# Routing table built from one comparison per tile with the token number multiplied in on ScalarE, late shared tiles ahead of the first expert sums, and context values loaded behind the second tile's rows

## The chip, the cores and the metric

One core of one Trainium2 chip runs the whole program in a single launch. The metric is device time in microseconds (us), the median of three runs. Every matrix lies in the on-chip memory with 128 partitions; TensorE (PE) multiplies, VectorE (DVE), ScalarE (ACT) and GpSimd (POOL) do the rest, SyncE (SP) issues most of the plain transfers, and POOL issues the indirect ones (gathers by a table of row numbers).

## The reference

The input x is 8 batches of 256 tokens with 256 features, so 2048 tokens. Four residual layers follow one another:

```
x = x + tanh(g_xattn[0]) * cross_attention(layernorm(x), context, mask)       (8 heads, 77 keys)
x = x + tanh(g_ffn[0])   * mixture(layernorm(x))                              (below)
x = x + tanh(g_xattn[1]) * self_attention_with_context(layernorm(x), context) (16 heads, 77 + 256 keys)
x = x + tanh(g_ffn[1])   * lora_mixture(layernorm(x))                         (8 experts, 2 a token)
```

The mixture of the second line has 64 experts of inner width 176. Each token takes 8 of them, by sigmoid scores and a choice of groups; its result is the weighted sum of their 8 outputs plus the output of one shared expert of width 352. The reference computes it densely; the kernel computes only the chosen experts.

## The kernel before, in words

Work is in tiles of 128 tokens: NT = 16 tiles, TOPK = 8 choices a token, so 128 pairs of a tile and a choice. The stages that the change touches are these.

**Shared expert, early part.** The first NSE = 10 tiles of tokens go through the shared expert while the routing table is being made. One step per tile (`s_step`) on PE: two up products (one for each half f of the inner width), the two transposes of the hidden values of the tile before, the transposes of the next tile's input, and the down product of the tile before. ACT does the silu and two copies of each half, copies hT (the transposed hidden values) and xT (the transposed input), and scales the down product into yC (`s_y_out`, line 1034). POOL multiplies silu and up values (`shared_h`) and adds yC to x.

**Routing table.** Each of the 2048 x 8 choices has got a slot number; slot / 128 is a block (one expert's batch of 128 rows), slot % 128 a place in it. The table idx (place x block -> token number) is made with matmuls: for a tile t and choice k, PE adds ohP^T x ohB to one PSUM bank. ohB (128 tokens x 192 blocks, fp16) is 1 where the token's block is, made for all 8 choices by one comparison (line 2083). ohP (128 tokens x 128 places, fp16) holds the token number where the token's place is, made by 8 instructions that compare and multiply (line 2088). These have a ring of OHS = 4 tiles: DVE can be at most four tiles ahead of PE, which counts each of its 128 matmuls on `b_ohu`. On PE the order is written out by hand: two tiles of the table behind each of the shared steps 6 to 9 (FILL_AT = 6), then transposes of the last hidden tile, table tile 8, the last down product, and tiles 9 to 15. When the bank is whole, three DVE instructions turn it into idx (lines 2097 to 2099), `b_idx` is raised, and POOL starts gathering (line 769).

**Routed experts.** 191 blocks, one step each (`c_step`): POOL gathers 128 rows of the normalised input by idx, PE transposes, multiplies up, transposes, multiplies down, ACT stores y to memory. SP loads the experts' weights into 8 slots as they come free.

**Late part.** The last NSL = 6 tiles of tokens go through the shared expert behind the last block, in 12 half steps m = 0 to 11 (`late_up`, `late_silu`, `c_hidden`, `late_down`); `late_hidden` on DVE does the product hC (line 2116) and the copy hT (line 2119) of the half steps that it is given, and `late_add` adds the finished tile into x (line 2150). When every y row is in memory POOL gathers, for each token tile, its 8 rows (line 786, yg): first 16 gathers for both tiles of batch 0, then 5 for batch 1. DVE sums the 8 rows (`d_reduce`, line 2247, two halves of a tile) and adds them into x (`d_sum`). Then come the statistics and the norm (`d_ve`, `d_rstd`, `d_norm`) with which the third layer starts. The order on DVE is written by hand: half steps 0 and 1, bproj, clearing half of qP (line 2395), 2 and 3, the other half, 4 and 5, and then by `FIRST_LATE` half steps between the four `d_reduce` of batch 0.

On SP the third layer's loads follow the last late row load: `load_raw(0)`, `load_raw(1)` (512 KB each), `load_keys(0)` (308 KB), a wait for cleared v1 and qP, `load_values(0)` and `load_values(1)` (two transfers each, in pieces of 64 bytes, line 628), `load_keys(1)`, which waits for POOL to have used the keys before, and more. PE first needs the values in `d_values` of batch 0.

qP and v1 are also cleared earlier, in six pieces during the first blocks (`clear`, lines 2123 to 2129), each of which counts on `d_zero`.

Of the kernel before, what the change touches and what calls it, by code (L numbers as in the profile page):

```python
# [14 lines left out]
P = 128  # L15
# [80 lines left out]
def bass_flamingo(nc, A, out):  # L96
    with ExitStack() as ctx:  # L97
# [5 lines left out]
        def sem(name):  # L103
            return ctx.enter_context(nc.semaphore(name))
# [44 lines left out]
        with ExitStack() as region:  # L149
# [32 lines left out]
            blkH = s("blkH", [P, NT * TOPK, 2], FP16)  # L182
            parF = s("parF", [P, NT * TOPK])
            iotaP = s("iotaP", [P, P], FP16)
# [109 lines left out]
        with ExitStack() as region:  # L294
# [23 lines left out]
        b_slot = sem("b_slot")  # L318
        b_sel, b_pos, b_eb, b_er, b_oh, b_ohu, b_idx = (
            sem(n) for n in ("b_sel", "b_pos", "b_eb", "b_er", "b_oh", "b_ohu", "b_idx"))  # L320

# [196 lines left out]
        def _(sp):  # L518
# [105 lines left out]
            def load_values(b):  # L624
                if b >= 2:
                    sp.wait_ge(d_pv, H1 * (b - 1))
                for e in range(2):
                    sp.dma_start(v1[0:NKEY, b % 2, 0, :, 3 * e, :], A["ctx"][b][:, D:2 * D].rearrange("k (p e d) -> e k p d", p=HP1, e=2)[e]).then_inc(d_cv[b % 2], 16)
# [15 lines left out]
            load_keys(0)  # L644
            sp.wait_ge(d_zero, ZERO_PIECES)
            load_values(0)
            load_values(1)
# [326 lines left out]
        def _(act):  # L974
# [81 lines left out]
            s_copy_xT(0, 0)  # L1056
            pairs(act, s_step, n=NSE)
            s_copy_hT(NSE - 1)
            s_y_out(NSE - 1, 1, NSE // 2 - 1)


# [205 lines left out]
        def _(pe):  # L1267
# [144 lines left out]

            def onehots(t, r):
                for k in range(TOPK):
                    pe.wait_ge(b_oh, TOPK * t + k + 1)
                    start = isinstance(t, int) and t == 0 and k == 0
                    stop = isinstance(t, int) and t == NT - 1 and k == TOPK - 1
                    mm(ps[:, POS[1], 0:NBLK], ohP[:, r, k, :], ohB[:, r, k, :], start, stop).then_inc(b_ohu, 1)

# [415 lines left out]
        def _(dve):  # L1835
# [239 lines left out]
            own.link(dve.tensor_scalar(slotI[:], slotI[:], P - 1, None, ALU.bitwise_and))  # L2075
            own.step(dve.tensor_copy(parF[:], slotI[:]))
            own.link(dve.tensor_copy(blkH[:], blkI[:].unsqueeze(2).broadcast_to([P, NT * TOPK, 2])))
            TWOS = [P, TOPK, NBLK // 2, 2]
            end()

            def onehots(t, r):
                after(dve, b_ohu, TOPK * (t - OHS + 1))
                dve.tensor_tensor(ohB[:, r, :, :].rearrange("p k (n a) -> p k n a", a=2),
                                  iotaB[:].rearrange("p (n a) -> p n a", a=2).unsqueeze(1).broadcast_to(TWOS),
                                  blkH[:, bass.ds(TOPK * t, TOPK), :].unsqueeze(2).broadcast_to(TWOS), ALU.is_equal)
                for k in range(TOPK):
                    u = TOPK * t + k
                    dve.tensor_scalar(ohP[:, r, k, :], iotaP[:], col(parF, u), col(id1, t), ALU.is_equal, ALU.mult).then_inc(b_oh, 1)

            for t in range(OHS):  # L2090
                onehots(t, t)
            with dve.Fori(1, NT // OHS) as i:
                for r in range(OHS):
                    onehots(OHS * i + r, r)
            dve.wait_ge(b_ohu, TOPK * NT)
            begin()
# [296 lines left out]
            dve.tensor_scalar(bproj[:], bproj[:], tg[:, 1:2], None, ALU.mult).then_inc(d_gate, 1)  # L2393
            for h in range(2):
                dve.memset(qP[h * (P // 2):(h + 1) * (P // 2), :, 1 - h, :].bitcast(F32), 0.0).then_inc(d_zero, 1)
                late_hidden(2 * h + 2, 2 * h + 3)

            FIRST_LATE = ((6, 7), (), (8, 9), (10, 11))
            for r in range(TB):
# [171 lines left out]
```

## Time and profile before

| what | us |
|---|---|
| median of 3 runs | 1512.27 (1512.11 to 1514.17) |
| the profiled execution, its own time | 1514.72 |
| its span in the trace | 1512.9 |
| PE busy | 1364.1 (90%) |
| DVE busy | 861.2 (57%) |
| ACT busy | 692.9 (46%) |
| POOL busy | 514.6 (34%) |
| mean granted TensorE clock | 0.943 of full |

The stages by the trace's clock: first attention to about 104 us, routing and early shared tiles to 216 us, routed blocks to about 715 us, late shared tiles and expert sums to 775 us, third layer to about 1200 us, fourth layer to the end. "Granted clock" 1.00 is 2.4 GHz and 0.50 is 1.2 GHz. A stretch in which PE is busy for all of its time says little about DVE; where PE has gaps, the engine that ends each gap sets the time.

### The profile page before, as it was taken

The page shows a single profiled execution, that of the slowest core. Times are in us where ns is not written, and L with a number is a line of the kernel's source. Part 1 is how long each engine was busy: PE and PEld are TensorE (multiplying, and loading weights), DVE is VectorE, ACT ScalarE, POOL GpSimd, SP SyncE. Part 2 cuts the span into 40 slices and gives each one's busy share as a digit, 9 for nine tenths or more (in the row PEclk, how much of TensorE's full clock was granted, in tenths as well). Part 3 has the DMA queues.
Part 4 walks back from the last instruction along what each step waited for, and adds up shares of the span by engine and source line. Part 5 has one row for each costly group of instructions (what it writes and reads, how often), then busy time and mean ns, then how long its engine had stood idle before and what let it go on. Part 6 is the DMA issues. An engine that isn't in the chain of part 4 may idle for free. (4 is left out here: it accounts for less than half of the span.)

```text
span 1512.9 us, 30501 instructions
## 1 busy us (share of the span) xinstructions
PE 1364.1 (90%) x8093; PEld 1070.4 (71%) x8093; DVE 861.2 (57%) x2301; ACT 692.9 (46%) x1847; POOL 514.6 (34%) x570
## 2 busy tenths in 40 slices
PE   4988969999999999999566799999998899999998
PEld 3876636777777777777344567776765799999997
DVE  6878964333333333333337567667678576666666
ACT  2444303444444444444024577677776444444443
POOL 1001323333333333331554477656662111111110
PEclk8877969999999999999787899999999899999999
DMA  4016115768566557643422122221120000000000
GB/s 104 0 54 170 26 33 161 219 191 241 160 202 185 174 161 218 192 115 93 128 86 64 57 57 65 59 66 50 44 87 22 10 13 15 15 14 14 14 7 15
DMA packets 107710, 136.12 MB, mean 90 GB/s; under 512 B 29843, under 2 KB 91635, under 8 KB 107603
## 3 DMA queue, kind: packets, MB, share of 16 engines
q1 hardware_dynamic: 64643, 61.15, 13.9%
q0 software_dynamic: 15456, 48.62, 12.0%
q10 hardware_dynamic: 27504, 25.05, 4.9%
q8 instruction: 53, 0.87, 0.2%
q14 instruction: 54, 0.44, 0.1%
HBM read 102.75 MB, written 32.01 MB: 89 GB/s over the span
## 5 line engine op out<-in xcount | busy, mean ns | idle before, releaser
L769 POOL DMA_INDIRECT xg<-n_rows,idx x191 | 181.1, 948 | 314.9 <-DVE wS L2110 218.5
L1269 PE MATMUL ps<-wgu,xT 128*128 x764 | 260.6, 464 | 0.6 <-ACT xT L1070 0.6
L1269 PE MATMUL ps<-wdn,hT 88*128 x764 | 198.4, 382 | 2.5 <-DVE hT L2119 2.5
L2287 DVE TENSOR_REDUCE nmx<-ps 128x1 f32<-128x333 f32 x256 | 127.1, 498 | 123.3 <-PE ps L1269 118.8
L1147 ACT ACTIVATE pD<-ps,nmx 128x333 f32<-128x333 f32 x256 | 139.2, 546 | 98.6 <-DVE nmx L2287 75.6
L2116 DVE TENSOR_TENSOR hC<-sg,ps 128x176 f32<-128x176 f32 x203 | 68.5, 337 | 185.1 <-ACT sg L1080 162.2
L2119 DVE COPY hT<-ps 88x256 f32<-88x256 f32 x203 | 85.4, 421 | 152.4 <-issue 86.9
L1269 PEld LDWEIGHTS ps<-wgu,xT 128*128 128x128 f32 x764 | 130.8, 191 | 42.5 <-issue 2.0
L1587 PE MATMUL ps<-ident,pD 128*128 128x128 f32 x768 | 130.9, 281 | 28.2 <-DVE pT L2293 16.0
L786 POOL DMA_INDIRECT yg<-y_rows,slotG x128 | 123.4, 964 | 93.3 <-ACT pD L1147 33.7
L1080 ACT ACTIVATE sg<-ps 128x176 f32<-128x176 f32 x191 | 60.6, 318 | 185.4 <-PE ps L1269 179.2
L1269 PEld LDWEIGHTS ps<-wdn,hT 88*128 88x128 f32 x764 | 130.8, 191 | 13.9 <-issue 3.0
L1089 ACT ACTIVATE yC<-ps,wS 128x256 f32<-128x256 f32 x191 | 90.6, 474 | 106.1 <-issue 65.8
L1587 PEld LDWEIGHTS ps<-ident,pD 128*128 128x128 f32 x768 | 98.8, 144 | 39.9 <-issue 21.0
L1269 PE MATMUL ps<-kM,qP 128*128 128x334 f32 x256 | 108.6, 426 | 5.2 <-ACT pD L1147 4.8
L1350 PEld LDWEIGHTS ps<-ident,xg 128*128 128x128 f32 x414 | 59.1, 144 | 64.8 <-issue 34.2
L1355 PE MATMUL ps<-ident,hC 128*88 128x128 f32 x446 | 85.6, 277 | 19.9 <-DVE hC L2116 13.9
L1269 PE MATMUL ps<-pT,v 128*32 128x256 f32 (+1 forms) x768 | 97.7, 390 | 0.6 <-ACT pT L1154 0.6
L2434 DVE TENSOR_TENSOR gg<-sl,ps 128x256 f32<-128x256 f32 x128 | 53.0, 420 | 79.3 <-ACT sl L1235 78.5
L1235 ACT ACTIVATE sl<-ps 128x256 f32<-128x256 f32 x128 | 48.3, 383 | 107.6 <-PE ps L1269 104.2
L1355 PEld LDWEIGHTS ps<-ident,hC 128*88 128x88 f32 x446 | 53.0, 124 | 53.9 <-DVE hC L2116 21.7
L1350 PE MATMUL ps<-ident,xg 128*128 128x128 f32 x414 | 80.7, 277 | 9.2 <-DMA xg<-n_rows,idx 6.1
(310 smaller groups left out, 3084.7 us busy)
## 6 DMA issues: line engine op xcount, KB each, us to landing
y_rows<-yC ACTq DMA_DIRECT2D x191, 128.0 KB
wgu<-in_wgu SPq DMA_DIRECT2D x64, 352.0 KB
wdn<-in_wdn SPq DMA_DIRECT2D x64, 176.0 KB
xg<-n_rows,idx POOLq DMA_INDIRECT x191
kraw<-in_kD SPq DMA_DIRECT2D x8, 308.0 KB
x<-in_x SPq DMA_DIRECT2D x4, 512.0 KB, 4.8
n_rows<-nB SPq DMA_DIRECT2D x4, 512.0 KB, 3.4
xg<-n_rows SPq DMA_DIRECT2D x16, 128.0 KB
```

The source lines that it names most:

```text
L769: pool.indirect_dma_start(out=xg[:, b % XS, :], out_offset=None, in_=n1_rows, in_offset=bass.IndirectOffsetOnAxis(ap=idx[:, b:b + 1], axis ...
L786: pool.indirect_dma_start(out=yg[:, q, k, :], out_offset=None, in_=y_rows, in_offset=bass.IndirectOffsetOnAxis(ap=slotG[:, u:u + 1], axis= ...
L1080: act.activation(sg[:, n % 2, :], ps[:, 2 + n % 2, 0:I0], ACT.Silu).then_inc(c_silu, 1)
L1089: act.activation(yC[:, (n - 1) % YS, :], ps[:, 6 + (n - 1) % 2, 0:D], ACT.Copy, scale=wS[:, (n - 1) % XS:(n - 1) % XS + 1]).then_inc(c_y, 1)
L1147: act.activation(pD[:, k % AHEAD, :], ps[:, score_bank(k), 0:NK1], ACT.Exp, bias=nmx[:, k:k + 1], accum_out=den[:, k // TB // HG1, head_of ...
L1269: return pe.matmul(o, lhsT, rhs, start=start, stop=stop, **kw)
L1350: last = pe.transpose(ps[:, bank, at + c * P:at + (c + 1) * P], xg[:, slot, c * P:(c + 1) * P], ident[:])
L1355: last = pe.transpose(ps[0:IC, bank, at + c * P:at + (c + 1) * P], hC[:, slot, c * IC:(c + 1) * IC], ident[:])
L1587: last = pe.transpose(ps[:, 5 + k % 2, c * P:(c + 1) * P], pD[:, k % AHEAD, at:at + P], ident[:])
L2116: dve.tensor_tensor(hC[:, n % 2, :], sg[:, n % 2, :], ps[:, 2 + n % 2, I0:GU], ALU.mult).then_inc(c_h, 1)
L2119: dve.tensor_copy(hT[:, n % 2, :, :], ps[0:IC, 4 + n % 2, 0:2 * P].rearrange("p (c n) -> p c n", c=2)).then_inc(c_hT, 1)
L2287: dve.tensor_reduce(nmx[:, k:k + 1], ps[:, score_bank(k), 0:NK1], AX, ALU.max, negate=True).then_inc(d_mx, 1)
```

## The change

Three edits. In the routing table the comparison of places is one DVE instruction for the 8 choices of a tile (`rows_of_a_tile`, 128 x 1024 fp16), ahead of the comparison of blocks; ACT multiplies the result in place by the token number (`numbered`, one instruction a tile, 128 x 1024 fp16, scale from id1). On ACT's queue two `numbered` stand behind each shared step 6 to 9, one behind the last hT copy, and the rest behind the last yC. PE waits once a tile for both, and counts once a tile. In the late part the two clearings of qP are gone, half steps 2 to 7 stand ahead of the first `d_reduce`, 8 behind the first, 9 to 11 behind the second, none behind the third and fourth. SP waits for the 8 gathers of batch 0's second tile (`k_ld[1]`) ahead of `load_values(0)`.

```diff
-            parF = s("parF", [P, NT * TOPK])
+            parH = s("parH", [P, NT * TOPK, 2], FP16)
...
             load_keys(0)
             sp.wait_ge(d_zero, ZERO_PIECES)
+            sp.wait_ge(k_ld[1], 16 * TOPK)
             load_values(0)
...
-            pairs(act, s_step, n=NSE)
+
+            def numbered(n):
+                rows = ohP[:, n % OHS, :, :].rearrange("p k n -> p (k n)")
+                act.wait_ge(b_oh, 2 * n + 1)
+                act.activation(rows, rows, ACT.Copy, scale=id1[:, n:n + 1]).then_inc(b_ohn, 1)
+
+            for t in range(2):
+                s_step(t, t, 0)
+            with act.Fori(1, FILL_AT // 2) as i:
+                for r in range(2):
+                    s_step(2 * i + r, r, i)
+            for t in range(FILL_AT, NSE):
+                s_step(t, t % 2, t // 2)
+                for s in range(2):
+                    numbered(2 * (t - FILL_AT) + s)
             s_copy_hT(NSE - 1)
+            numbered(2 * (NSE - FILL_AT))
             s_y_out(NSE - 1, 1, NSE // 2 - 1)
+            for n in range(2 * (NSE - FILL_AT) + 1, NT):
+                numbered(n)
...
             def onehots(t, r):
+                pe.wait_ge(b_oh, 2 * t + 2)
+                pe.wait_ge(b_ohn, t + 1)
                 for k in range(TOPK):
-                    pe.wait_ge(b_oh, TOPK * t + k + 1)
...
-                    mm(ps[:, POS[1], 0:NBLK], ohP[:, r, k, :], ohB[:, r, k, :], start, stop).then_inc(b_ohu, 1)
+                    last = mm(ps[:, POS[1], 0:NBLK], ohP[:, r, k, :], ohB[:, r, k, :], start, stop)
+                last.then_inc(b_ohu, 1)
...
-            own.step(dve.tensor_copy(parF[:], slotI[:]))
+            own.step(dve.tensor_copy(parH[:], slotI[:].unsqueeze(2).broadcast_to([P, NT * TOPK, 2])))
...
+            def rows_of_a_tile(out, iota, number, t, n):
+                twos = [P, TOPK, n // 2, 2]
+                return dve.tensor_tensor(out.rearrange("p k (n a) -> p k n a", a=2),
+                                         iota[:].rearrange("p (n a) -> p n a", a=2).unsqueeze(1).broadcast_to(twos),
+                                         number[:, bass.ds(TOPK * t, TOPK), :].unsqueeze(2).broadcast_to(twos), ALU.is_equal)
+
             def onehots(t, r):
-                after(dve, b_ohu, TOPK * (t - OHS + 1))
-                dve.tensor_tensor(ohB[:, r, :, :].rearrange("p k (n a) -> p k n a", a=2),
...
-                for k in range(TOPK):
-                    u = TOPK * t + k
-                    dve.tensor_scalar(ohP[:, r, k, :], iotaP[:], col(parF, u), col(id1, t), ALU.is_equal, ALU.mult).then_inc(b_oh, 1)
+                after(dve, b_ohu, t - OHS + 1)
+                rows_of_a_tile(ohP[:, r, :, :], iotaP, parH, t, P).then_inc(b_oh, 1)
+                rows_of_a_tile(ohB[:, r, :, :], iotaB, blkH, t, NBLK).then_inc(b_oh, 1)
...
-            for h in range(2):
-                dve.memset(qP[h * (P // 2):(h + 1) * (P // 2), :, 1 - h, :].bitcast(F32), 0.0).then_inc(d_zero, 1)
-                late_hidden(2 * h + 2, 2 * h + 3)
-
-            FIRST_LATE = ((6, 7), (), (8, 9), (10, 11))
+            late_hidden(2, 3, 4, 5, 6, 7)
+
+            FIRST_LATE = ((8,), (9, 10, 11), (), ())
```

## Rows read from the trace of the kernel before

**Rows 1.** Busy time by stretch: us, then PE, PEld, DVE, ACT, POOL, granted clock, DMA share, GB/s
```profile
200.00:212.00 12.00, 8.39 (x36) 3.75 (x36) 12.00 (x43) 0.00 (x0) 0.00 (x0) 0.50 0.01 1
320.00:700.00 380.00, 374.38 (x1791) 274.35 (x1790) 123.13 (x449) 158.68 (x447) 139.24 (x147) 1.00 0.61 180
732.00:740.00 8.00, 3.83 (x14) 2.23 (x13) 2.54 (x3) 0.32 (x1) 5.86 (x8) 0.94 0.94 281
740.00:748.00 8.00, 2.91 (x8) 1.63 (x6) 0.81 (x2) 0.00 (x0) 6.17 (x7) 0.50 0.57 132
```
**Rows 2.** Groups by line and form: count | busy us, mean ns | idle before
```profile
L2088 DVE TENSOR_SCALAR ohP<-iotaP,parF,id 128x128 f16<-128x128 f16 x128 | 33.7, 332 | 0.0
...
L2083 DVE TENSOR_TENSOR ohB<-iotaB,blkH 128x1536 f16<-128x1536 f16 x16 | 15.4, 961 | 0.0
...
L1175 ACT CAST lT_h<-maskS 128x1024 fp32r<-128x1024 f32 x8 | 8.3, 1040 | 1.0 <-DVE maskS L2347 1.0
...
L1034 ACT ACTIVATE yC<-ps,tg 128x256 f32<-128x256 f32 x10 | 4.7, 474 | 14.7 <-PE ps L1269 14.7
...
L1102 ACT COPY xT<-ps 128x256 f32<-128x256 f32 x6 | 2.2, 372 | 0.0
```
**Rows 3.** Timeline of PE, 172 to 213 us: start, us, what, [idle before]
```profile
172.39 2.65 PE L1269 MATMUL ps<-wguS,xT 128*128 128x352 f32 x4
...
178.89 1.49 PE L1269 MATMUL ps<-ohB,ohP 128*128 128x192 f16 x16
180.21 1.38 PE L1269 MATMUL ps<-wguS,xT 128*128 128x352 f32 x4
...
184.99 1.49 PE L1269 MATMUL ps<-ohB,ohP 128*128 128x192 f16 x16
...
192.20 0.60 PE L1355 MATMUL ps<-ident,hC 128*88 128x128 f32 x4
...
193.90 1.97 PE L1269 MATMUL ps<-wdnS,hT 88*128 88x256 f32 x8
...
211.22 1.90 PE L1269 MATMUL ps<-ohB,ohP 128*128 128x192 f16 x8 [0.75 <-DVE ohP L2088]
```
**Rows 4.** Timeline of ACT at the start of the table
```profile
166.88 0.47 ACT L1034 ACTIVATE yC<-ps,tg 128x256 f32<-128x256 f32 x1 [1.24 <-PE ps L1269]
```
**Rows 5.** Timeline of DVE at the end of the table
```profile
213.16 0.36 DVE L2097 TENSOR_SCALAR isz<-ps 128x192 f32<-128x192 f32 x1 [0.43 <-PE ps L1269]
```
**Rows 6.** Timeline of POOL: the first block gather; the first and 21st row gather
```profile
216.14 1.10 POOL L769 DMA_INDIRECT xg<-n_rows,idx  x1 [18.29 <-issue]
...
722.32 0.95 POOL L786 DMA_INDIRECT yg<-y_rows,slotG  x1 [28.52 <-DMA y_rows<-yC]
...
747.40 0.95 POOL L786 DMA_INDIRECT yg<-y_rows,slotG  x1 [0.30 <-issue]
```
**Rows 7.** Timeline of DVE in the late part
```profile
721.04 1.76 DVE L2395 MEMSET qP<- 64x2048 f32 x1 [0.37 <-issue]
722.73 0.27 DVE L2116 TENSOR_TENSOR hC<-sg,ps 128x176 f32<-128x176 f32 x1
...
746.07 0.42 DVE L2119 COPY hT<-ps 88x256 f32<-88x256 f32 x1 [7.63 <-remote]
...
753.46 1.87 DVE L2247 TENSOR_REDUCE ysum<-yg 128x128 f32<-128x1024 f32 x1
...
769.33 0.48 DVE L2150 SCALAR_TENSOR_TENSOR x<-ps,tg,x 128x256 f32<-128x256 f32 x1 [1.22 <-PE ps L1269]
```
**Rows 8.** Timeline of ACT in the late part and in the third layer
```profile
751.68 0.32 ACT L1109 ACTIVATE sg<-ps 128x176 f32<-128x176 f32 x1 [13.70 <-remote]
...
828.06 0.48 ACT L1154 COPY pT<-ps 128x384 f32<-128x384 f32 x1 [4.94 <-remote]
```
**Rows 9.** Timeline of SP, the value loads
```profile
733.38 6.69 SPq L628 DMA_DIRECT2D v<-in_ctx  x4
```
**Rows 10.** DMA of 740 to 744 us: SP's queue q1: packets, MB, share of 16 engines
```profile
q1 hardware_dynamic: 1314, 0.08, 23.1%
```

More of the change, by code:

```diff
@@ L318, in bass_flamingo @@
         b_slot = sem("b_slot")
-        b_sel, b_pos, b_eb, b_er, b_oh, b_ohu, b_idx = (
-            sem(n) for n in ("b_sel", "b_pos", "b_eb", "b_er", "b_oh", "b_ohu", "b_idx"))
+        b_sel, b_pos, b_eb, b_er, b_oh, b_ohn, b_ohu, b_idx = (
+            sem(n) for n in ("b_sel", "b_pos", "b_eb", "b_er", "b_oh", "b_ohn", "b_ohu", "b_idx"))
         s_x = [sem(f"s_x{r}") for r in range(2)]
@@ L2075, in _ @@
             own.link(dve.tensor_scalar(slotI[:], slotI[:], P - 1, None, ALU.bitwise_and))
-            own.step(dve.tensor_copy(parF[:], slotI[:]))
+            own.step(dve.tensor_copy(parH[:], slotI[:].unsqueeze(2).broadcast_to([P, NT * TOPK, 2])))
             own.link(dve.tensor_copy(blkH[:], blkI[:].unsqueeze(2).broadcast_to([P, NT * TOPK, 2])))
-            TWOS = [P, TOPK, NBLK // 2, 2]
             end()
-            def onehots(t, r):
-                after(dve, b_ohu, TOPK * (t - OHS + 1))
-                dve.tensor_tensor(ohB[:, r, :, :].rearrange("p k (n a) -> p k n a", a=2),
-                                  iotaB[:].rearrange("p (n a) -> p n a", a=2).unsqueeze(1).broadcast_to(TWOS),
-                                  blkH[:, bass.ds(TOPK * t, TOPK), :].unsqueeze(2).broadcast_to(TWOS), ALU.is_equal)
-                for k in range(TOPK):
-                    u = TOPK * t + k
-                    dve.tensor_scalar(ohP[:, r, k, :], iotaP[:], col(parF, u), col(id1, t), ALU.is_equal, ALU.mult).then_inc(b_oh, 1)
+            def rows_of_a_tile(out, iota, number, t, n):
[3 more added lines that the diff above has]
+                                         number[:, bass.ds(TOPK * t, TOPK), :].unsqueeze(2).broadcast_to(twos), ALU.is_equal)
+            def onehots(t, r):
+                after(dve, b_ohu, t - OHS + 1)
+                rows_of_a_tile(ohP[:, r, :, :], iotaP, parH, t, P).then_inc(b_oh, 1)
+                rows_of_a_tile(ohB[:, r, :, :], iotaB, blkH, t, NBLK).then_inc(b_oh, 1)
             for t in range(OHS):
@@ L2094, in _ @@
                     onehots(OHS * i + r, r)
-            dve.wait_ge(b_ohu, TOPK * NT)
+            dve.wait_ge(b_ohu, NT)
             begin()
```

## The prediction

> **What bounds the kernel now.** I read the busy times by stretch first, then each engine's timeline around the two edited places, then the groups for prices, and last the DMA.
>
> The routed blocks between the two places are PE's: 374 of 380 us busy at full clock [rows 1]. Their 12 matmuls a block (1791 in 380 us) make a step of about 2.5 us. They start when the first gather starts, and everything behind them waits for them. So a microsecond won ahead of the first gather at 216.14 [rows 6] is won at the end, as is one won between the last block and the start of the third layer.
>
> In the routing table DVE sets the end: from 200 to 212 us it is busy for all 12 us, ACT for none, and PE, at half clock, waits before each tile for ohP [rows 1, 3]. A tile costs DVE one ohB and 8 ohP. The last matmuls start at 211.22 and run 1.90, so PE is done at 213.12 and DVE goes on at 213.16 [rows 3, 5]. Earlier, however, PE and not DVE is the pace: while shared steps run, the sixteen matmuls of two tiles run without a wait in 1.49 us, and one turn (step and two tiles) takes 184.99 - 178.89 = 6.10 us [rows 3]. DVE is up to four tiles ahead there. Its 47 us of comparisons are thus on the path only in the tail.
>
> In the late part nothing is busy: PE 2.91 of 8 us in 740 to 748, ACT none [rows 1]. The last half step's add is at 769.33 [rows 7]. The waits that matter bear no engine's name: ACT stands 13.70 us before the silu at 751.68 and DVE 7.63 us before the copy at 746.07, both "remote", both waiting for PE matmuls long issued [rows 7, 8]. They fall into the 21 gathers that POOL issues from 722.32 to 747.40 at 1.25 us each [rows 6], and into the time in which the DMA engines are 0.94 busy [rows 1].
>
> **The change, part by part: the table.** On DVE the 8 instructions of 332 ns fall away: 33.7 + 15.4 = 49.1 us busy over 16 tiles is 3.1 us a tile now [rows 2]. One instruction of 1024 elements comes. Its nearest row is ohB, the same form with 1536 elements in 961 ns [rows 2]. In proportion that is 0.64 us, and it can't be more than the 0.96 of the larger one; I take 0.65. A tile then costs DVE about 1.6 us. The preparation cast grows from 128 to 256 outputs, below 0.1 us. A rule of the Trainium skill speaks against this edit: VectorE: DVE Perf Modes, "The perf-mode tier table", says that a 16-bit operation on two tensors makes two results a cycle where a tensor_scalar makes four. By it alone the new comparison would be the slower one for each element. The 332 ns for 128 elements show that most of the old price was a fixed part paid eight times.
>
> On ACT the product comes, 128 x 1024. The nearest row is the cast of 1024 elements, 1040 ns; a scale read from a column adds 474 - 372 = 0.10 us [rows 2], so 1.14, and 1.05 at the pitch of one behind another. That those rows are 32-bit leaves a bound below: half of it, 0.57, if 16-bit data ran twice as fast. The Trainium skill (ScalarE: Activation LUTs, "What ACT_TABLE_LOAD costs") gives 0.833 ns an element for fp32 and bf16 alike, and about 93 ns for each column operand, which would make 1.13.
>
> Now the path, on PE and ACT together. **Start:** ACT is free at 166.88 + 0.47 = 167.35 [rows 4]. Two products: 168.5 and 169.55. PE needs 0.66 for the second eight matmuls (half of 1.49, less the tail), so shared step 7 starts at 170.2 instead of 172.39 [rows 3]: -2.2 us. **Three turns (steps 7, 8, 9):** the products stand on ACT behind the yC that needs PE's down product, so when PE has ended the step it waits 0.5 for yC, 1.14 and 1.05 for two products, and runs 0.66 more: 3.4 us in place of the 1.33 between the start of the sixteen and the next step. +2.1 each, +6.2 us. The cover under which the comparisons ran is given up here: DVE's time is not saved in these turns, since PE did not wait for it. **Tail:** from the transposes at 192.20 to 213.12 it is 20.9 us [rows 3]. Then: transposes 0.45, hT copy 0.6, product 1.14, eight matmuls 0.66, down product 1.8, yC 0.5, product 1.14, six more at 1.05, last eight 0.66, and four handovers of 0.15: 13.9. That is at full clock. At half clock, which rows show for this stretch before (0.50 in 200 to 212, [rows 1]), the eight matmuls take 1.3 us a tile and become the pace of the last seven: 2.1 more, 16.0. I take the half clock, as PE stands still for as long as before: -4.9 us. DVE's ring of four leaves 1.6 + 1.14 + 1.3 a tile round a loop of four tiles, no bound. Sum of the table: -2.2 + 6.2 - 4.9 = **-0.9 us**.
>
> **The late part.** Each clearing stands 1.76 us in DVE's queue and makes the hC behind it wait: the one at 721.04 ends where hC starts at 722.73 [rows 7], which at the steps' pitch would have started some 1.2 us sooner. Twice 1.2 us. qP is zero already and bproj stays, so nothing else moves with them. That puts PE and DVE one half step of 2.5 us ahead when the long waits start at about 733. If these stay as they are, DVE has half step 8 at 752 where it had 7. Behind it: 1.1 us for step 8, the second reduce with its sum and statistics 2.7 (a reduce is 1.87 us, [rows 7]), 9 to 11 at 2.5 each less what overlaps, about 6, and the last two reduces with sum and statistics 4.6. I come to the last add at 767.4 instead of 769.3 + 0.5: **-2.4 us**. The reduces no longer stand between the half steps, but they are still DVE's work.
>
> The four value transfers take SP 6.69 us from 733.38 [rows 9] and lie among the row gathers. Alone in 740 to 744 they take 23.1% of the engines, 0.9 us, for 0.08 MB in 1314 packets [rows 10]; I put as much again for the 4 us before, by the same number of pieces. Moved behind the second tile's gathers, they give back **1.7 us** of a full DMA. At their new place, about 745, they need some 10 us and are waited for by the first `d_values`, beyond 800. On SP the load_keys(1) behind them waits anyway for POOL at about 774, and the next loads stand behind that, so the wait costs nothing unless the late part ends 15 us earlier.
>
> Total: -0.9 - 2.4 - 1.7 = -5.0 us. The sum is made against the profiled execution, 1514.72 us (span 1512.9 and 1.8 around it). That is 2.4 above the median of the three runs, 1512.27. So 1507.3. About 0.2%, 3 us, is what a measurement of this kernel can tell from no change.
>
> **Rivals.** (a) *The long waits go.* If the value packets are what holds PE's results between 733 and 752, the half steps run on at 2.5 us, end at about 749, and the second tile's rows (last gather issued at about 741, landed by 745) set the last two reduces: the add at about 754, -15.5 us instead of -4.1, total -16, so 1496. For it: the waits fall into the fullest DMA. Against it: ACT waits 4.94 us "remote" before 828.06 [rows 8] while only gathers run, and the wait up to 751.68 has 8 us behind the last value packet. The gathers alone make such waits. 0.14.
>
> (b) *It cancels.* The products behind yC cost what the tail gives, the late part gives the 2.4 us and the third layer's start eats some of it, where POOL's next eleven gathers hold PE again. 1512.3 less 0 to 3. 0.28.
>
> (c) *Slower.* PE's gap of 2.7 us after each shared step, split by eight matmuls, lets the clock fall to 0.50 during steps 7 to 9. The up product at 172.39 takes 2.65 us at half clock, the one at 180.21 takes 1.38 [rows 3]; over the part of a step that runs before the clock is back I put 1.7 us. With all three +5, the table is at +4.2 and the whole at 0; it is slower from there if the late part gives less than 2, for instance because the values now collide with the last five gathers and hold PE in half steps 9 to 11: 1512.3 + 4. For it: PE is idle more than a quarter of each turn. Against: each gap stands beside 4.8 us without one (6.10 - 1.33), and step 7 was slow before as well. The Trainium skill, TensorE: Matmul & The Clock Gate, names 1.2 GHz as the state after idling; it gives (c) its mechanism. 0.11.
>
> (d) *The comparison is not made at the fast rate* because of its broadcast operands: ohB has the same and took 961 ns for 1536, so I leave it out.
>
> **How the numbers follow.** My forecast, -3 to -9, has 0.47; (a) 0.14, (b) 0.28, (c) 0.11. Faster by over 3 us: nearly all of the forecast case and (a), 0.58. Within: 0.30. Slower: 0.12. The range takes in the bounds: the tail at full clock (-2.1 more), 16-bit products at 0.57 us (-8), and on the other side the clock's fall (+5). 1498 to 1514.
>
> **What would show it.** Right: ohP as one instruction of about 0.65 us, product 1.14 us, gap on PE of about 1.65 us before table tiles 2, 4, 6 with ACT's product as releaser; first block gather at about 215; ACT's wait before 752 still there; last late add about 767 less the table's gain. Wrong: a first gather before 212 (products cheaper, or overlapped) or after 218 (clock), or the "remote" waits gone.

## The result: slower by 0.33% where 0.3% faster was forecast

The changed kernel takes 1519.47 us (median of 6, 1516.63 to 1521.99), the kernel before, run beside it, 1513.41 (6 runs, 1512.11 to 1515.30): ratio 1.0033, 95% interval 1.0020 to 1.0046. The forecast was 1507.3 within 1498 to 1514, so both the sign and the range are wrong. The profiled execution is the lowest of the six, 1516.63 with a span of 1514.9; against the 1512.9 of before the two traces hold 2.0 us of the 6.1 by which the medians differ. By stage: everything ahead of the table is 2.5 us shorter (DVE's first comparison at 163.57, before 166.04), the table 3.1 longer, the way from the first block gather to the third layer's first norm (nS) 0.6 shorter, and what stands behind it 2.0 longer (741.4, before 739.4). The edits leave the last of these alone and touch the first by one cast, so what the two executions differ by there can't be laid to them.

Busy time by stretch of the changed kernel (columns as in [rows 1]), and the head of its page:

```profile
200.00:212.00 12.00, 9.47 (x57) 8.18 (x58) 5.79 (x8) 7.45 (x9) 0.72 (x1) 0.68 0.01 1
320.00:700.00 380.00, 374.32 (x1793) 274.63 (x1792) 123.12 (x448) 159.05 (x449) 138.86 (x147) 1.00 0.61 180
732.00:740.00 8.00, 4.39 (x12) 2.41 (x12) 0.34 (x1) 0.32 (x1) 6.09 (x7) 0.59 0.68 245
740.00:748.00 8.00, 2.07 (x4) 1.17 (x4) 0.81 (x2) 0.00 (x0) 6.14 (x9) 0.50 0.59 118
```
```profile
span 1514.9 us, 30328 instructions
...
PE 1357.9 (90%) x8093; PEld 1070.2 (71%) x8093; DVE 835.3 (55%) x2187; ACT 709.1 (47%) x1863; POOL 512.6 (34%) x570
```

DVE has 26 us less to do (861.2 before), and nothing came of it. The routed blocks are the same. In the table DVE is no longer busy all the time, but the end did not come earlier. In 740 to 748 us there is still next to nothing at work.

Groups by line and form in 160 to 216 us of the changed kernel (count | busy us, mean ns | idle before):

```profile
L2102 DVE TENSOR_TENSOR ohB<-iotaB,blkH 128x1536 f16<-128x1536 f16 x16 | 15.7, 983 | 0.0
L2102 DVE TENSOR_TENSOR ohP<-iotaP,parH 128x1024 f16<-128x1024 f16 x16 | 11.0, 686 | 24.0 <-PE ps L1287 23.8
```
```profile
L1062 ACT ACTIVATE ohP<-ohP,id 128x1024 f16<-128x1024 f16 x16 | 17.3, 1139 | 1.1 <-DVE ohP L2102 1.1
```

The prices were right: 0.69 us for the comparison (0.65 forecast), 1.14 for the product (1.14). The 24 us of idle time in front of the comparisons, released by PE, say that DVE's saving has become waiting. PE's timeline shows why:

```profile
165.71 0.83 PE L1287 MATMUL ps<-ohB,ohP 128*128 128x192 f16 x8 [2.20 <-DVE ohB L2102]
...
167.59 1.44 PE L1287 MATMUL ps<-ohB,ohP 128*128 128x192 f16 x8 [1.04 <-ACT ohP L1062]
168.82 2.61 PE L1287 MATMUL ps<-wguS,xT 128*128 128x352 f32 x4
...
172.07 2.11 PE L1287 MATMUL ps<-wguS,xT 128*128 128x352 f32 x4
...
177.82 0.82 PE L1287 MATMUL ps<-ohB,ohP 128*128 128x192 f16 x8 [1.69 <-ACT ohP L1062]
178.85 0.82 PE L1287 MATMUL ps<-ohB,ohP 128*128 128x192 f16 x8 [0.22 <-ACT ohP L1062]
179.51 1.38 PE L1287 MATMUL ps<-wguS,xT 128*128 128x352 f32 x4
...
186.15 0.82 PE L1287 MATMUL ps<-ohB,ohP 128*128 128x192 f16 x8 [1.69 <-ACT ohP L1062]
187.19 1.41 PE L1287 MATMUL ps<-ohB,ohP 128*128 128x192 f16 x8 [0.22 <-ACT ohP L1062]
188.39 2.50 PE L1287 MATMUL ps<-wguS,xT 128*128 128x352 f32 x4
...
197.76 1.06 PE L1373 MATMUL ps<-ident,hC 128*88 128x128 f32 x4
200.62 1.44 PE L1287 MATMUL ps<-ohB,ohP 128*128 128x192 f16 x8 [1.81 <-ACT ohP L1062]
201.86 3.13 PE L1287 MATMUL ps<-wdnS,hT 88*128 88x256 f32 x8
206.68 0.82 PE L1287 MATMUL ps<-ohB,ohP 128*128 128x192 f16 x8 [1.69 <-ACT ohP L1062]
207.72 6.02 PE L1287 MATMUL ps<-ohB,ohP 128*128 128x192 f16 x48 [0.22 <-ACT ohP L1062]
```

Each turn ends with 1.69 us for the product behind yC and 0.22 for the second, as forecast. From the up product of step 7 to the last transposes it is now 197.76 - 168.82 = 28.9 us, 19.8 before (172.39 to 192.20, [rows 3]): +9.1. The waits make 3 x 1.91 = 5.7 of that. Another 0.3 a turn goes because the sixteen matmuls no longer run close behind the down product and one another (a turn's waits thus cost 2.2). The other 2.5 us are the granted clock at half: 0.7 in step 7's second up product (2.11 us, 1.42 before), 0.6 in the eight matmuls at 187.19 (1.41 us, 0.82 at 178.85), 1.1 in the up product at 188.39 (2.50 us, 1.38 at 179.51 for the same four matmuls) and 0.1 behind 196.97. From the transposes to the end at 213.74 it is 16.0 us, as forecast. From DVE's first comparison (163.57, before 166.04) to isz it is 50.2 us where it was 47.1.

The two ends of the table and the late part, timelines of DVE, POOL and ACT of the changed kernel:

```profile
163.57 0.69 DVE L2102 TENSOR_TENSOR ohP<-iotaP,parH 128x1024 f16<-128x1024 f16 x1
164.18 1.48 DVE L2102 TENSOR_TENSOR ohB<-iotaB,blkH 128x1536 f16<-128x1536 f16 x1
...
213.78 0.36 DVE L2118 TENSOR_SCALAR isz<-ps 128x192 f32<-128x192 f32 x1 [1.42 <-PE ps L1287]
...
741.19 0.42 DVE L2140 COPY hT<-ps 88x256 f32<-88x256 f32 x1 [7.02 <-remote]
...
749.95 0.34 DVE L2137 TENSOR_TENSOR hC<-sg,ps 128x176 f32<-128x176 f32 x1 [7.95 <-ACT sg L1127]
...
751.48 1.88 DVE L2268 TENSOR_REDUCE ysum<-yg 128x128 f32<-128x1024 f32 x1
754.47 0.34 DVE L2137 TENSOR_TENSOR hC<-sg,ps 128x176 f32<-128x176 f32 x1 [1.11 <-ACT sg L1127]
...
764.80 3.66 DVE L2268 TENSOR_REDUCE ysum<-yg 128x128 f32<-128x1024 f32 x2
...
769.36 0.47 DVE L2171 SCALAR_TENSOR_TENSOR x<-ps,tg,x 128x256 f32<-128x256 f32 x1
```
```profile
216.76 1.10 POOL L770 DMA_INDIRECT xg<-n_rows,idx  x1 [10.45 <-issue]
...
746.47 0.95 POOL L787 DMA_INDIRECT yg<-y_rows,slotG  x1 [0.30 <-issue]
```
```profile
733.49 0.32 ACT L1127 ACTIVATE sg<-ps 128x176 f32<-128x176 f32 x1 [5.36 <-remote]
749.60 0.32 ACT L1127 ACTIVATE sg<-ps 128x176 f32<-128x176 f32 x1 [15.80 <-remote]
```

One more line of DVE before, which no row shows, and PE's up product of half step 7 in the changed kernel:

```profile
736.32 1.87 DVE L2247 TENSOR_REDUCE ysum<-yg 128x128 f32<-128x1024 f32 x1 [2.46 <-DMA yg<-y_rows,slotG]
```
```profile
734.68 2.55 PE L1287 MATMUL ps<-wguS,xT 128*128 128x352 f32 x4
```

The half steps run 2.4 us apart up to half step 5, earlier than before, and then stand in longer remote waits: 15.80 us where it was 13.70 [rows 8]. PE has done the up product of half step 7 at 737.2, and ACT starts its silu at 749.60, 12.4 us later. The lead goes in two places. In the wait it falls from 4.9 us (hT of half step 6 at 741.19, before 746.07 [rows 7]) to 2.1 (hC of half step 7 at 749.95, before 752.03). Behind the wait those 2.1 go too: before, one of the four sums was done inside the wait, at 736.32, and hC of half step 7 is followed by the last add 17.3 us later; now all four stand behind it, from 751.48 on, and it is 19.4 (e7 and e6, the old order and the new on another chip, have 18.5 and 20.6). The last add is at 769.36, before 769.33 [rows 7].

### The profile page after: what moved, and what is told of

It is laid out like the page before. It is cut to its first block and busy times, and to the rows that moved or that the text cites. A ratio compares the mean times of both kernels' runs of the same rounds, so it can differ in the third digit from the quotient of the medians.

```text
span 1514.9 us, 30328 instructions
## 1 busy us (share of the span) xinstructions
PE 1357.9 (90%) x8093; PEld 1070.2 (71%) x8093; DVE 835.3 (55%) x2187; ACT 709.1 (47%) x1863; POOL 512.6 (34%) x570
## 5 line engine op out<-in xcount | busy, mean ns | idle before, releaser
L1373 PEld LDWEIGHTS ps<-ident,hC 128*88 128x88 f32 x446 | 53.3, 125 | 50.9 <-DVE hC L2137 16.5
```

Of the source, the lines that this page charges most:

```text
L1373: last = pe.transpose(ps[0:IC, bank, at + c * P:at + (c + 1) * P], hC[:, slot, c * IC:(c + 1) * IC], ident[:])
```

## The experiments

Five sets of three or four kernels ran, each set on one chip and beside its own runs of the kernel before. Two sorts of chip were met, and nothing can be understood without them. On chips of sort W the kernel before takes 1513 to 1517 us and the traces have the long remote waits; the first result and sets 2 and 4 (two chips) are of this sort. On chips of sort F it takes 1483 us and no trace has a remote wait on ACT or DVE in the late part or the third layer; sets 1, 3 and 5 (two chips, 1 and 5 the same one). Ratios are against the kernel before on the same chip.

| run | set, sort | this, before (median us) | ratio (95%) |
|---|---|---|---|
| e1_table | 1 F | 1486.63, 1483.41 | 1.0026 (1.0014 to 1.0039) |
| e2_late | 1 F | 1474.64 | 0.9940 (0.9925 to 0.9955) |
| e3_values | 1 F | 1481.88 | 0.9989 (0.9979 to 1.0000) |
| e4_ahead | 1 F | 1467.74 | 0.9896 (0.9878 to 0.9914) |
| e5_changed | 2 W | 1521.84, 1516.51 | 1.0045 (1.0031 to 1.0059) |
| e6_late_values | 2 W | 1519.12 | 1.0012 (0.9995 to 1.0028) |
| e7_clearings | 2 W | 1517.82 | 1.0007 (0.9995 to 1.0019) |
| e8_order | 2 W | 1515.08 | 0.9996 (0.9983 to 1.0009) |
| e9_paced | 3 F | 1484.93, 1483.46 | 1.0008 (0.9997 to 1.0019) |
| e10_ahead_again | 3 F | 1466.62 | 0.9883 (0.9869 to 0.9897) |
| e11_ahead_paced | 3 F | 1471.06 | 0.9911 (0.9898 to 0.9924) |
| e12_changed_again | 4 W | 1517.31, 1513.77 | 1.0026 (1.0016 to 1.0036) |
| e13_paced_later | 4 W | 1510.95 | 0.9981 (0.9970 to 0.9992) |
| e14_ahead_table | 4 W | 1503.59 | 0.9930 (0.9915 to 0.9946) |
| e15_ahead_third | 4 W | 1500.14 | 0.9908 (0.9893 to 0.9924) |
| e16_changed_third | 5 F | 1481.96, 1482.75 | 0.9994 (0.9981 to 1.0007) |
| e17_ahead_paced_five | 5 F | 1468.98 | 0.9901 (0.9881 to 0.9920) |
| e18_ahead_fourth | 5 F | 1466.23 | 0.9879 (0.9855 to 0.9903) |

Two stretches of each profiled run tell the parts apart: the table, from DVE's first comparison to isz, and the way from the first block gather to nS. Each figure is of one execution.

| kernel | table | gather to nS, sort F | gather to nS, sort W |
|---|---|---|---|
| old table, old late part | 47.1 (before, e3, e7); 46.8 (e8) | 543.6 (e3, later values) | 557.3 (before), 558.1 (e7, no clearings), 559.2 (e8, new order) |
| changed table, old late part | 49.3 (e1) | 543.4 (e1) | |
| new late order | 47.0 (e2) | 538.5 (e2) | |
| new late order and values | 46.8 (e6) | 536.7 (e16) | 556.7 (changed), 557.7 (e12), 558.9 (e5), 561.9 (e6) |
| changed table in the changed kernel | 50.2, 49.9 (e5), 49.9 (e12), 50.9 (e16) | | |
| products one step ahead | 36.5, 35.6 (e4, e10), 36.4 (e14), 35.3 (e15), 36.2 (e18) | 537.0, 538.1, 535.4 (e4, e10, e18) | 556.9 (e15), 559.1 (e14, old late part) |
| paced gathers | | 539.7 (e9), 539.7 (e11), 537.5 (e17) | 545.4 (e13) |

### One part alone (e1, e2, e3)

The table's edit alone is the change without its hunk on SP and without the last one. The late order alone:

```diff
-            for h in range(2):
-                dve.memset(qP[h * (P // 2):(h + 1) * (P // 2), :, 1 - h, :].bitcast(F32), 0.0).then_inc(d_zero, 1)
-                late_hidden(2 * h + 2, 2 * h + 3)
-            FIRST_LATE = ((6, 7), (), (8, 9), (10, 11))
+            late_hidden(2, 3, 4, 5, 6, 7)
+            FIRST_LATE = ((8,), (9, 10, 11), (), ())
```

The values alone are one line on SP, `sp.wait_ge(k_ld[1], 16 * TOPK)`, ahead of `load_values(0)`.

> The kernel before with the routing table's edit alone (one comparison for the eight place rows, the products on ScalarE, PE waiting once a tile); the late order, its two clearings and the value loads as before. Theory A (the loss is in the table): in the profile of the changed kernel the table takes 50.2 us from the first comparison to the sums' end, against 47.1 before, so this kernel is 3 to 4 us slower than the kernel before, about 1516.5. Theory B (the table cancels, as I predicted, -0.9, and the loss is in the late part): within 1 us of the kernel before, 1512 to 1513.5.

> The kernel before with the late order alone: no second clearing of the queries' buffer, all late half steps up to 7 ahead of the first sums, 8 behind the first sum, 9 to 11 behind the second. Theory A (the late part is nearly neutral, since the profile of the changed kernel has its last add 0.9 us later behind the last block's product than before): 0 to +1.5 us, 1513 to 1515. Theory B (the late part holds the loss, because both sums of the second tile now stand behind the half steps that wait longest, at 764.80 for 3.66 us): +3 to +6 us. My prediction had -2.4.

> The kernel before with the later value loads alone. Theory A (the long waits go with the row gathers that POOL issues back to back and not with the value pieces): -1.7 to +0.5 us, with ACT's wait of over 10 us before about 750 still there. Theory B (the value pieces now collide with the last gathers or with the third layer's first loads, and this holds the loss): +2 to +4 us. My prediction had -1.7.

e1: ratio 1.0026, which is +3.9 us, and the table took 49.3 us. Theory A of e1 holds: this edit costs 3 to 4 us by itself (the absolute times in the expectations of this set are those of a chip of sort W). e2: 8.9 us faster, which neither theory had. On this chip the half steps of the late part are not held by anything but the queue of DVE. With the old order (e1), half step 6 stands behind a sum that waits for its rows:

```profile
729.72 1.87 DVE L2267 TENSOR_REDUCE ysum<-yg 128x128 f32<-128x1024 f32 x1 [4.21 <-DMA yg<-y_rows,slotG]
731.51 0.33 DVE L2136 TENSOR_TENSOR hC<-sg,ps 128x176 f32<-128x176 f32 x1
...
754.24 0.48 DVE L2170 SCALAR_TENSOR_TENSOR x<-ps,tg,x 128x256 f32<-128x256 f32 x1 [1.22 <-PE ps L1286]
```

With the new one two more half steps are done by then, and the last add comes at 750.06 in e2 though the first gather was 0.7 us later. The way to nS is 4.9 us shorter than in e1, 5.1 than in e3. The other 3.8 us of the 8.9 lie in no stretch that the trace explains: the profiled execution took 1478.5 us, the longest of e2's five. e3: -1.6 us, interval -3.1 to 0, where I had -1.7.

### The changed kernel on both sorts of chip (e5, e12, e16), and the late edits on sort W (e6, e7, e8)

e5, e12 and e16 are the changed kernel as it is. e6 is the kernel before with the late order and the values; e7 is the kernel before and leaves out only the two memsets; e8 keeps them and changes only the order:

```diff
+            late_hidden(6, 7)
-            FIRST_LATE = ((6, 7), (), (8, 9), (10, 11))
+            FIRST_LATE = ((8,), (9, 10, 11), (), ())
```

> The changed kernel itself, unaltered, beside new runs of the kernel before. The experiments on single parts ran on a chip on which the kernel before takes 1483.4 us and shows no wait of kind remote. Theory A (the parts add up: table +3.2, late order -8.8, values -1.5): 7 us faster than the kernel before on such a chip, and on a chip where the kernel before takes about 1513 us and shows the long remote waits, slower by about 6 as measured at first. Theory B (the parts collide with one another, whatever the chip): 4 to 6 us slower than before here too.

> The changed kernel once more, unaltered, to have it on the other kind of chip. Theory A (the parts add up): on a chip where the kernel before takes 1483 us, 7 us faster than it, 1476 to 1477, with all half steps 2.4 us apart and no remote wait; on a chip where it takes 1513 to 1516, +5 to +6 again. Theory B (the parts collide whatever the chip): slower than before on either.

> The changed kernel unaltered. Theory A (the parts add up on a chip without remote waits, where the kernel before takes 1483 us): about 1477, and the table alone takes 50 us there too. On a chip with them: +3.5 to +6 once more. Theory B (the sum does not hold): within 3 us of the kernel before, or slower, on a chip without remote waits.

> The late order and the later value loads together, the table as before. Theory A (the parts add up): -10.4 us on a chip without the remote waits; on a chip with them, +1 to +3, so that the table's +3.8 and this make the +6 measured at first. Theory B (the two late edits collide, since the values now wait for gathers that the late steps need too): clearly less than the sum of the two alone, -4 or worse.

> The kernel before without the second clearing of the queries' buffer, the late half steps in the old places. Theory A (each clearing held a half step for 1.2 us, as I predicted): -2 to -3 us. Theory B (DVE would wait there anyway for the first gathered rows): 0 to -1 us.

> The kernel before with the two clearings kept and only the order changed: half steps 6 and 7 ahead of the first sum, 8 behind it, 9 to 11 behind the second. Theory A (in the old order the half step behind a sum waits for the gathered rows, 4 us at 729 in a chip without remote waits, so the order carries most of the late gain): -5 to -7 us on such a chip, about 0 on a chip with remote waits. Theory B (the clearings carry it): 0 to -2 us.

On sort W the loss is there each time: +5.0, +6.8, +3.9 us by the ratios (about +6 was expected of e5, which holds, and +5 to +6 of e12, which came out a little lower). Beside the old table the late edits win nothing there: +1.8 (-0.8 to +4.2) together, as expected of e6, +1.1 (-0.8 to +2.9) the memsets, where both theories of e7 had a gain, -0.6 (-2.6 to +1.4) the order, as expected of e8, and gather to nS stays at 556.7 to 561.9. So on sort W the table's loss is what is left (3.1 us in the first trace, +3.9 by e1), with what e6 may add. One pair says otherwise: e14 and e15 below, one chip of sort W, differ only in the late edits, and with them it is 3.4 us less (1498.7 to 1501.4 against 1500.5 to 1505.0). Whether these edits win or lose up to 3 us on sort W is open; the 4.1 us that I forecast they do not win. On sort F the changed kernel comes to -0.9 us (-2.8 to +1.0), no change that can be told, where theory A of e16 had -6. Its late part did what e2's did: the first sum waits 2.32 us, and all is done at 750:

```profile
733.16 1.87 DVE L2268 TENSOR_REDUCE ysum<-yg 128x128 f32<-128x1024 f32 x1 [2.32 <-DMA yg<-y_rows,slotG]
734.95 0.33 DVE L2137 TENSOR_TENSOR hC<-sg,ps 128x176 f32<-128x176 f32 x1
...
750.07 0.47 DVE L2171 SCALAR_TENSOR_TENSOR x<-ps,tg,x 128x256 f32<-128x256 f32 x1
```

The medians of the parts do not add up there (+3.9 - 8.9 - 1.6 = -6.6 against -0.9), but the traces do. Between e1, which has the changed table, and e16, on the same chip, the way to nS is 6.7 us shorter (543.4, 536.7) and the table 1.6 longer (49.3, 50.9), so -5.1; e1 itself stands at +3.9, which makes -1.2. The term that is too large is e2's -8.9, of which its trace explains 5; where its median comes from stays open.

### The products one step ahead (e4, e10, e15, e18; with the old late part e14)

```diff
                 s_step(t, t % 2, t // 2)
-                for s in range(2):
-                    numbered(2 * (t - FILL_AT) + s)
+                for n in range(4) if t == FILL_AT else range(2 * (t - FILL_AT) + 2, 2 * (t - FILL_AT) + (3 if t == NSE - 1 else 4)):
+                    numbered(n)
             s_copy_hT(NSE - 1)
-            numbered(2 * (NSE - FILL_AT))
+            numbered(2 * (NSE - FILL_AT) + 1)
+            numbered(2 * (NSE - FILL_AT) + 2)
             s_y_out(NSE - 1, 1, NSE // 2 - 1)
-            for n in range(2 * (NSE - FILL_AT) + 1, NT):
+            for n in range(2 * (NSE - FILL_AT) + 3, NT):
                 numbered(n)
```

> The changed kernel with ScalarE's products moved one shared step ahead: four behind step 6, and behind each later step's output scaling the two of the next step, so that they run while PE does this step's tiles and the next up product; in the tail three of them ahead of the last output scaling. Theory A (what the table lost is PE's wait for the products at the end of each turn, 1.69 + 0.22 us, and the clock that falls with it): turns are back to about 6.1 us, PE's wait before tiles 2, 4, 6 is gone, the sums end at 196 to 202 instead of 213.8, and the kernel comes to 12 to 17 us below the changed kernel, 1502 to 1507. Theory B (the start of the gathers is not set by the sums but by something else that ends at about 213, or the products are the bound anyway): less than 4 us gained.

> The kernel before with the table's edit and its products one step ahead, the late order and the values as before. Theory A (the table by itself, with PE never waiting for a product during the shared steps, takes 36 us from the first comparison where the kernel before takes 47.1): 10 to 11 us below the kernel before, on either kind of chip. Theory B (part of the gain of the combined kernel came from the late order): less than 8.

> The products one step ahead in the changed kernel, for the third time, to have it on the other kind of chip. Theory A: on a chip with remote waits 13 to 14 us below the changed kernel, 8 to 9 below the kernel before; on one without, 15.7 to 16.8 below the kernel before as measured twice. Theory B (the earlier start is given back in the remote waits): within 4 us of the kernel before.

PE's timeline of e15, sort W:

```profile
169.36 2.18 PE L1288 MATMUL ps<-wguS,xT 128*128 128x352 f32 x4
...
176.27 1.38 PE L1288 MATMUL ps<-wguS,xT 128*128 128x352 f32 x4
...
181.05 1.49 PE L1288 MATMUL ps<-ohB,ohP 128*128 128x192 f16 x16
182.38 1.38 PE L1288 MATMUL ps<-wguS,xT 128*128 128x352 f32 x4
...
186.94 1.49 PE L1288 MATMUL ps<-ohB,ohP 128*128 128x192 f16 x16
...
198.18 0.82 PE L1288 MATMUL ps<-ohB,ohP 128*128 128x192 f16 x8 [0.65 <-ACT ohP L1062]
```

A turn is back to 6.1 us, the sixteen matmuls run in 1.49 without a wait, of the up products only step 7's first, at 169.36, is slow (2.18 us), and the table ends at 199.0. It takes 35.3 us instead of 49.9 in e12 on the same chip: 14.6. The kernel is 17.2 us below the changed one and 13.6 below the kernel before, more than the 13 to 14 and 8 to 9 expected of e15 (e4's sums ended at 202.0, at the late end of what was expected); e14 makes -10.6 (-12.9 to -8.2) by the table alone, as expected. On sort F it is 15 to 18 below the kernel before, three times (e10 and e18 were expected at -15.7 and at -14 to -17). That the same instructions at the same prices, only placed elsewhere on ACT's queue, turn +3 into -11 shows that the loss was PE's wait and the clock behind it. This version beats both kernels on both sorts of chip.

### Pacing the gathers (e9, e11, e13, e17)

POOL's gathers of the second tile wait for PE's half steps, one each; e9 and e11 also hold back the five for the third tile until the last half step, e13 moves them behind the context keys, e17 lets them follow:

```diff
-            gather_y(0, 0)
+            gather_y(0, 0, range(1))
+            for k in range(TOPK):
+                pool.wait_ge(c_th, NRUN + 4 + k)
+                gather_row(0, 0, 1, k)
```

> The changed kernel with POOL's gathers of the second tile paced by PE: gather k waits until the transposes of late half step 3 + k are done, and the five gathers for the third tile wait for the last half step. Nothing is left out. Theory A (gathers that POOL issues one right behind another are what holds back PE's completions, on chips where they are held): on such a chip, where the changed kernel takes about 1520 us, the remote waits of 5 to 16 us between 730 and 751 shrink to under 5 us and the last late add comes at 750 to 758 instead of 769 to 771, 12 to 18 us faster than the changed kernel, so 10 to 13 below the kernel before; on a chip without remote waits it changes at most 1 us. Theory B (something else makes the waits, such as the landing of the rows or stores): the waits stay, and since the gathers then come later the kernel is 3 to 10 us slower than the changed one.

> Both: the products one step ahead and the paced gathers. Theory A (each mends its own place): the sum of the two, about 24 us below the kernel before on a chip with remote waits, and about 16 below on one without. Theory B (something else takes over): less than the better of the two alone.

> The changed kernel with the second tile's gathers paced by PE as in the first paced kernel, but the five for the third tile moved behind the context keys instead of behind the last half step, so that POOL's power for the third layer's first norm does not wait for them. Theory A (gathers issued one right behind another hold back PE's completions): on a chip with remote waits these shrink to under 5 us each and the kernel is 10 to 18 us below the changed one; on one without, within 2 us of the changed one. Theory B: the waits stay as long, and nothing is gained.

> The changed kernel with the products one shared step ahead and with the second tile's gathers paced by PE's late half steps; the five gathers for the third tile follow right behind. Theory A (the two mends are in different places and add up): on a chip with remote waits about 6 us below the kernel with the products ahead alone, so about 20 below the kernel before; on one without, 0 to 2 us above the kernel with the products ahead alone. Theory B (the gathers held back now crowd the third layer's start): no gain over it on a chip with remote waits.

Only e13 met a chip of sort W. ACT's and POOL's timelines there:

```profile
735.03 0.32 ACT L1128 ACTIVATE sg<-ps 128x176 f32<-128x176 f32 x1 [6.05 <-remote]
```
```profile
741.22 0.95 POOL L787 DMA_INDIRECT yg<-y_rows,slotG  x1 [2.15 <-PE ps L1374]
...
748.59 0.95 POOL L787 DMA_INDIRECT yg<-y_rows,slotG  x1 [3.43 <-PE ps L1374]
```

And ACT's of e12, the changed kernel on the same chip:

```profile
752.17 0.32 ACT L1127 ACTIVATE sg<-ps 128x176 f32<-128x176 f32 x1 [15.08 <-remote]
```

While eleven gathers still run back to back, up to 735, there is a remote wait of 6.05 us. From the first spaced one at 738 on there is none on ACT until 776, and hC of half step 8 is at 743.1 where e12 waited 15.08 us and had that of half step 7 at 752.5. From gather to nS it is 545.4 us instead of 557.7. Theory A's mechanism holds: a run of gathers that POOL issues 1.25 us after one another is what PE's completions are held back behind on these chips. The value loads also moved (to 753.8, from 745.7 in e12), but e12's waits had begun at 737 without them. Not told apart is whether the issuing or the rows being moved does it, since spacing the one spaces the other.

The size was missed: 10 to 18 us below the changed kernel were expected, and of the 12.3 us 6.4 are left at the end. All sixteen gathers of the next pair now stand in one run from 763.6 to 783.5, DVE's maximum waits 15.9 us for PE behind it (10.8 in e12), and from nS to the end it is 745.1 us instead of 740.4. On sort F there is no wait to mend, and pacing costs: e11 is 4.4 us above e10 and e17 2.8 above e18, and e9 is at +1.2 against the kernel before where the changed kernel was at -0.9 (at most 1 us was expected of e9, up to 2 of e17, and of e11 theory B came true). Whether pacing and the products ahead add up on sort W was not measured, since e17 met sort F.

## Why the prediction was wrong, point by point

**Prices on DVE and ACT**: right (0.69 and 1.14 us). The rival that the comparison is not fast was rightly left out. Beside a POOL instruction it is slower, as DVE's and POOL's timelines of e4 show:

```profile
178.98 1.03 DVE L2103 TENSOR_TENSOR ohP<-iotaP,parH 128x1024 f16<-128x1024 f16 x1 [3.74 <-PE ps L1288]
...
180.81 0.68 DVE L2103 TENSOR_TENSOR ohP<-iotaP,parH 128x1024 f16<-128x1024 f16 x1
```
```profile
178.74 0.73 POOL L736 TENSOR_TENSOR x<-x,yC 128x256 f32<-128x256 f32 x1 [1.30 <-ACT yC L1035]
```

It takes 1.03 us where an add that began before it still runs for 0.49 us, and 0.68 where POOL stands still until its last 0.1 us. The Trainium skill (SBUF — State Buffer, "SBUF: two separate sides") says that a DVE instruction with two inputs in SBUF and a GpSimd instruction that reads SBUF hold one pair of ports exclusively, whichever starts first; the trace agrees, with 0.35 us lost.

**Start, -2.2 us**: mis-sized. Counted from DVE's first comparison, step 7 begins after 5.25 us (163.57 to 168.82) instead of 6.35 (166.04 to 172.39): -1.1. I took ohP for the only thing to wait for; PE waited 2.20 us for ohB, whose first instance took 1.48 us instead of 0.95, with an add of POOL's in 164.10 to 164.84. The other half of the miss is the clock: the second eight matmuls ran at half (1.44 us, 0.82 at full).

**Three turns, +6.2**: they cost +9.1. The waits came as worked out, 1.69 + 0.22 each, and cost 2.2 a turn where I had 2.1. The step that failed is the clock, a term that my sum put at nothing: I put its fall into a rival, with 1.7 a turn and a chance of 0.11, and it happened. Step 7's second up product, eight of the matmuls behind step 8 and the first up product of step 9 ran at half clock, 2.5 us in all.

**Tail, 16.0 us**: right in sum, by luck in its makeup. I had the last tiles' matmuls at half clock as the pace; they came 1.04 us a tile at ACT's pace, and it was the transposes at 197.76 (1.06 us), the eight matmuls at 200.62 (1.44) and the down product (3.13) that ran at half and made up for it. Sum of the table: -1.1 + 9.1 - 4.9 = +3.1 against -0.9; of the 4.0 between them, 3.1 are the clock. It was visible beforehand that the new work needed no place behind yC; I costed the order as given and set a gain in the tail against a loss in the turns, two large terms with a small difference, and took it for sure enough to leave the sign to the late part.

**Late order, -2.4**: 0 in the first result (last add at 769.36, before 769.33). The sentence that failed is "If these stay as they are, DVE has half step 8 at 752 where it had 7". The waits did stay, but they are not a pause of fixed length that begins at 733 for whoever comes: half step 7 comes out of them just behind the end of POOL's run of gathers, whatever was done before. In all nine traces of sort W with gathers in one run, hC of half step 7 stands 27.8 to 30.6 us behind the first row gather, whose run is 26 us long; on sort F it is 11.3 in the new order and 19.6 to 19.9 in the old (e2, e3, e1). So DVE had half step 8 at 754.47. From there to the end of the last add it took 15.4 us, just what 752 and 767.4 leave (the terms that I gave for it add up to 14.4). What I also missed is that the old order used the wait for one of the four sums and the new one puts all four behind it. Where the waits are missing the same edit was worth 5 us, twice what I had.

**Values, -1.7**: -1.6 in e3 on sort F (up to 0 within its interval); alone it was not run on sort W, where with the late order it gave no gain (e6). The place that I argued from does not show it: with the later loads (e3) the way to nS is 543.6 us, without them (e1) 543.4. So the size may be luck, and what it comes from is open.

**Rival (a)**: refuted. SP issued the value loads only from 742.97 on, DVE had waited 7.02 us by 741.19 all the same, and ACT's wait grew from 13.70 to 15.80 us. Its counter-argument, that the gathers alone make such waits, is what e13 shows. **(b)**, cancels, is what happens on sort F; its reasons (table even, late part held) are not those. **(c)** was nearest: its table at +4.2 against +3.1 to +3.9 is right, its clock fell at half the price that I gave it in the turns (2.5 us for 5), and its collision of the values is not seen. It should have had the larger chance, since the slow up product at 172.39 spoke for it. The Trainium skill (TensorE: Matmul & The Clock Gate, "Part 1: The HAM clock gate") names 1.2 GHz as the state after idling; the trace agrees in so far as the eight matmuls at 187.19 and the up product at 188.39 ran at half clock behind PE's waits.

**The signs named**: ohP, product and the 1.65 us gap came as said; the first gather at 216.76 lay within my "neither right nor wrong" although the table was slower, since the stages ahead ended 2.5 us earlier in that execution. A mark by the trace's clock should be counted from an event of the same stage.

## What to carry to other kernels

When work is taken from an engine that runs ahead and given to one whose queue is tied to the bound engine, its place in that queue decides: one shared step earlier, the same sixteen products turned +3 us into -11. Before counting on a lead, look at what ends the next long wait; if that is a run of transfers on another queue and not a duration, the lead ends there, and work that could have been done inside the wait is best left in it. Where two large terms nearly cancel, give both signs an even chance.

## What the runs showed of the hardware

The same kernel takes 1483 us on some chips and 1513 to 1517 on others, 2%, at a mean granted clock of 0.955 and 0.946. From the first block gather to nS, with the late part of before, it is 543.4 us on sort F (e1) and 557.3 on W (before), and behind nS 722 to 730 against 739 to 745, so about half of the difference lies in the layers behind the change. The remote waits are only on W: PE's results reach ACT up to 12.4 us late (the up product that ends at 737.2 in the changed kernel) while POOL issues indirect gathers every 1.25 us, and the long waits are gone where these stand 2.4 to 4.4 us apart (e13). What in those chips makes it is not known from these runs; two chips of each sort ran, and the first result's. The late order is thus worth 5 us in the traces of one sort of chip and nothing that can be told on the other, and a comparison must stay on one chip.
